# Causal attention in a one-core block: scores from two fp32r parts, two heads in the two halves of the array, and the causal mask as 64-row matmuls

## The reference

```python
xn = _layernorm(x)                                   # x: 4096 tokens x 256
normed = _layer_norm(xn, ln1_g, ln1_b)
q, k, v = normed @ Wqkv + bqkv                       # 16 heads of 16
q, k = rope(q), rope(k)
scores = einsum('bhqd,bhkd->bhqk', q, k) / 4         # causal, 4096 x 4096 per head
attn_out = softmax(scores) @ v
x1 = xn + attn_out @ Wo + bo
s = x1 + gelu(layer_norm(x1) @ W1 + b1) @ W2 + b2
g = silu(moe(xn))                                    # 8 experts, at most 512 rows each, and a shared network
out = x + s * g
```

## Time and profile before

| | us |
|---|---|
| median of 3 runs | 2709.79 |
| lowest and highest | 2703.81, 2711.1 |
| span of the profiled execution, first to last instruction | 2663.3 |
| PE, DVE, ACT, POOL busy | 2394.4, 2072.5, 1463.1, 377.9 |

### The profile page before, as it was taken

The page is one execution under the profiler, slowest core; times in us unless marked ns, Lnnn a source line. Parts: engine busy times, 40 slices in busy tenths (PEclk is TensorE's granted clock), DMA queues, the critical chain, the costliest instruction groups (busy, mean ns, idle before and its releaser), DMA issues. The chain is left out here.

```text
span 2663.3 us, 49751 instructions
## 1 busy us (share of the span) xinstructions
PE 2394.4 (90%) x14968; PEld 1211.4 (45%) x14968; DVE 2072.5 (78%) x3856; ACT 1463.1 (55%) x1762; POOL 377.9 (14%) x319
## 2 busy tenths in 40 slices
PE   0999947999999999998899999999999868886998
PEld 0889942333333333232333333333322247776888
DVE  7888889999999988562799999988864257776776
ACT  2444513566666666777566666666677733332443
POOL 2111149500000000000000000000000023333344
PEclk9999977999999999999999999999999979998999
DMA  4122247300000021000410000003100144443232
GB/s 123 64 95 91 90 114 186 104 9 9 9 9 1 9 50 43 13 10 17 92 30 9 9 9 9 1 9 70 28 9 9 22 115 126 126 126 97 64 95 71
DMA packets 158629, 144.79 MB, mean 54 GB/s; under 512 B 36448, under 2 KB 142176, under 8 KB 158304
## 3 DMA queue, kind: packets, MB, share of 16 engines
q1 hardware_dynamic: 155360, 133.94, 18.9%
q0 software_dynamic: 3072, 8.39, 0.9%
HBM read 95.61 MB, written 46.66 MB: 53 GB/s over the span
## 5 line engine op out<-in xcount | busy, mean ns | idle before, releaser
L883 DVE TENSOR_REDUCE attn_MX<-psB 128x1 f32<-128x512 f32 (+3 forms) x2352 | 1357.2, 638 | 352.5 <-PE psB L756 223.2
L869 ACT ACTIVATE attn_PB<-psB 128x1024 f32<-128x1024 f32 (+3 forms) x1152 | 1035.8, 950 | 563.9 <-PE psB L788 509.7
L756 PE MATMUL psB<-attn_KS,attn_QS 96*128 96x512 bf16 (+3 forms) x2352 | 764.5, 370 | 51.5 <-DVE attn_MX L883 44.9
L788 PE MATMUL psB<-attn_QS,attn_KS 104*128 104x512 bf16 (+3 forms) x2304 | 652.6, 363 | 24.5 <-ACT attn_QS L846 16.0
L803 PE MATMUL psB<-attn_PB,attn_V 128*32 128x512 f32 (+3 forms) x4608 | 579.8, 570 | 0.0
L756 PEld LDWEIGHTS psB<-attn_KS,attn_QS 96*128 96x128 bf16 x2352 | 200.6, 97 | 639.8 <-DVE attn_MX L883 522.2
L788 PEld LDWEIGHTS psB<-attn_QS,attn_KS 104*128 104x128 bf16 x2304 | 210.2, 98 | 336.1 <-ACT attn_PB L869 128.9
L1043 POOL TENSOR_TENSOR W1L<-W,W1H 128x512 fp32r<-128x512 f32 x36 | 53.8, 1524 | 1664.3 <-ACT W1H L1120 1664.3
L803 PEld LDWEIGHTS psB<-attn_PB,attn_V 128*32 128x32 f32 x4608 | 96.3, 108 | 175.9 <-issue 166.8
L759 PE MATMUL psB<-attn_mask_qk,attn_idb 128*128 128x128 bf16 x544 | 119.2, 227 | 0.0
L42 PE MATMUL ps_experts<-W2H,HH_experts 128*128 128x256 f32 x256 | 83.9, 328 | 35.1 <-DVE Y_experts L1233 20.3
(11 more groups left out here) (213 smaller groups left out, 3216.5 us busy)
## 6 DMA issues: line engine op xcount, KB each, us to landing
W<-in_w SPq DMA_DIRECT2D x18, 1024.0 KB, 5.5
attn_KS<-qk_parts SPq DMA_DIRECT2D x240, 64.0 KB, 3.7
attn_QS<-qk_parts SPq DMA_DIRECT2D x210, 64.0 KB, 2.8
qk_parts<-proj_PT SPq DMA_DIRECT2D x32, 384.0 KB, 3.3
attn_V<-v_rows SPq DMA_DIRECT2D x40, 256.0 KB, 4.8
v_rows<-proj_VA SPq DMA_DIRECT2D x32, 256.0 KB, 2.0
XI_experts<-rows_by_place SPq DMA_DIRECT2D x9, 512.0 KB, 6.3
AO_experts<-attention_sums SPq DMA_DIRECT2D x9, 512.0 KB, 6.7
```

The source lines that it names most:

```text
L756: mm = nc.tensor.matmul(ps[:, bank, 0:width], QS[0:MROW, i % 4, h, j * P:(j + 1) * P], KS[w][0:MROW, h, kc * CH:kc * CH + width], start=Tr ...
L788: mm = nc.tensor.matmul(ps[:, bank, r * P:CH], KS[w][0:KROWS, h, kb * P:(kb + 1) * P], QS[0:KROWS, i % 4, h, r * P:CH], start=True, stop=( ...
L869: nc.scalar.activation(PB[:, u % RING, 2 * pair:2 * pair + 2, r * P:CH], ps[:, 2 * (s % 2):2 * (s % 2) + 2, r * P:CH], ACT.Exp, scale=HD * ...
L883: nc.vector.tensor_reduce(MX[:, m % 4, HG * j + h, kc:kc + 1], ps[:, MB + off % 3, 0:w], AX.X, ALU.max).then_inc(reduced, 1)
```

## The change

Parts: q and k are cut into two fp32r parts instead of three bf16 ones, with one copy of ACT and one subtraction of DVE; a score is a sum of three products, 48 rows, and 4 rows for the maximum, 52 in all (`KROWS`). Even heads take rows 0 to 51 of the array, odd heads rows 64 to 115, each half with its own 4 rows for the maximum. The two matmuls of a pair in `scores` are now of two halves; consecutive jobs of maxima also alternate between the halves. The maximum's rows of `QS` are zero until they are set, by a DMA of zeros (two more DMAs in each `load_q`). The ones of `KS` come from a small tile by 8 DMAs instead of POOL. The mask is made by two 64-row bf16 matmuls of 64 columns for each head, in the head's half, instead of one of 128 rows and 128 columns. Jobs on the diagonal of 128 and (for c > 0) 256 keys are made for two heads at once, with one reduction. The constants `TERMS`, `TILE` replace `PAIRS`.

```diff
-PAIRS = ((0, 0), (0, 1), (1, 0), (1, 1), (0, 2), (2, 0))
-MROW = HD * len(PAIRS)
-KROWS = MROW + 2 * HG
+TILE = P // 2
+MROW, MROWS = 32, 4
+TERMS = ((0, 0, 0), (HD, 0, 1), (MROW + MROWS, 1, 0))
+KROWS = HD * len(TERMS) + MROWS
...
+def diagonal_jobs(c):
+    paired = TPC // 2 if c > 0 else 1
+    wide = [(j, (t, t + 2), c) for j in range(paired) for t in range(2)]
+    return wide + [(j, (h,), c) for j in range(paired, TPC) for h in range(HG)]
...
-                        if u < 4:
-                            dve.wait_ge(part1, 4 * c + u + 1)
...
-                            nc.vector.tensor_tensor(RS[:, u % 2, :], ps[:, QTB + u % 2, :], PT[:, u, 0, :], ALU.subtract).then_inc(rest1, 1)
-                        if u > 0:
-                            dve.wait_ge(part2, 4 * c + u)
-                            nc.vector.tensor_tensor(PT[:, u - 1, 2, :], RS[:, (u - 1) % 2, :], PT[:, u - 1, 1, :],
-                                                    ALU.subtract).then_inc(part3, 1)
...
+                        dve.wait_ge(high_made, 4 * c + u + 1)
+                        nc.vector.tensor_tensor(PT[:, u, 1, :], ps[:, QTB + u % 2, :], PT[:, u, 0, :].bitcast(F32),
+                                                ALU.subtract).then_inc(low_made, 1)
...
-        KS = [sb(f"KS{w}", [P, HG, N], BF16) for w in range(2)]
+        KS = [sb(f"KS{w}", [P, 2, N], F32R) for w in range(2)]
-        QS = sb("QS", [P, 4, HG, CH], BF16)
+        QS = sb("QS", [P, 4, 2, CH], F32R)
...
-                    for r, (a, _) in enumerate(PAIRS):
-                        sp.dma_start(QS[HD * r:HD * (r + 1), i % 4, :, :],
-                                     qk[a, 0, bass.ds(group, 1), :, :, c * CH:(c + 1) * CH].rearrange("g d h n -> (g d) h n")).then_inc(q_in[i % 4], 16)
+                    for t in range(2):
+                        for r, a, _ in TERMS:
+                            sp.dma_start(QS[TILE * t + r:TILE * t + r + HD, i % 4, :, :].bitcast(F32),
+                                         qk[a, 0, bass.ds(group, 1), t, :, :, c * CH:(c + 1) * CH].rearrange("g d b n -> (g d) b n")).then_inc(q_in[i % 4], 16)
+                        sp.dma_start(QS[TILE * t + MROW:TILE * t + MROW + MROWS, i % 4, :, :].bitcast(F32).rearrange("p b (x n) -> p (b x) n", n=D),
+                                     zeros_row).then_inc(q_in[i % 4], 16)
...
+                sp.wait_ge(ones_made, 4)
+                for w in range(2):
+                    for t in range(2):
+                        for b in range(2):
+                            sp.dma_start(KS[w][TILE * t + MROW:TILE * t + MROW + MROWS, b, :].bitcast(F32).rearrange("p (x n) -> p x n", n=P),
+                                         ONES[:, b:b + 1, :].broadcast_to([MROWS, NT, P])).then_inc(ones_in, 16)
...
-                for w in range(2):
-                    for c in range(NC):
-                        part = KS[w][MROW:KROWS, :, c * CH:(c + 1) * CH]
-                        nc.gpsimd.memset(part, 0.0).then_inc(consts, 1)
-                        for first in range(2):
...
-                            nc.gpsimd.affine_select(out=part, in_=part, compare_op=ALU.not_equal, fill=1.0, base=-HG * first,
-                                                    pattern=[[-1, HG], [0, CH]], channel_multiplier=1).then_inc(consts, 1)
...
+                    for at, h in enumerate(hs):
+                        rows, b = slice(TILE * (h % 2), TILE * (h % 2) + KROWS), h // 2
+                        mm = nc.tensor.matmul(ps[:, bank, at * width:(at + 1) * width], QS[rows, i % 4, b, j * P:(j + 1) * P],
+                                              KS[w][rows, b, kc * CH:kc * CH + width], start=(at == 0), stop=(kc < c))
...
+                    both = jobs[i % LS][at:at + 2]
+                    for n, job in enumerate(both):
+                        max_job(reads, i, off + n, job, used(n), q_need)
+                    for half in range(2):
+                        for n, job in enumerate(both):
+                            mm = hide_later_keys(off + n, job, half)
+                            if half == 1:
+                                mm.then_inc(maxed, 1)
...
-                    for b in range(2):
-                        h = 2 * pair + b
-                        bank = 2 * (s % 2) + b
-                        mm = nc.tensor.matmul(ps[:, bank, r * P:CH], KS[w][0:KROWS, h, kb * P:(kb + 1) * P],
-                                              QS[0:KROWS, i % 4, h, r * P:CH], start=True, stop=(kb < TPC * c))
-                        if kb >= TPC * c:
-                            mm = nc.tensor.matmul(ps[:, bank, r * P:(r + 1) * P], idb[:, :], mask_kq[:, :], start=False, stop=True)
+                    for t in range(2):
+                        rows = slice(TILE * t, TILE * t + KROWS)
+                        mm = nc.tensor.matmul(ps[:, 2 * (s % 2) + t, r * P:CH], KS[w][rows, pair, kb * P:(kb + 1) * P],
+                                              QS[rows, i % 4, pair, r * P:CH], start=True, stop=(kb < TPC * c))
+                    if kb >= TPC * c:
+                        for half in range(2):
+                            for t in range(2):
+                                rows = slice(TILE * t, TILE * (t + 1))
+                                mm = nc.tensor.matmul(ps[:, 2 * (s % 2) + t, r * P + TILE * half:r * P + TILE * (half + 1)],
+                                                      later_kq[half][rows, :], hide[rows, 0, :], start=False, stop=(half == 1))
```

191 lines of the change are left out of this document (102 added, 89 removed).

## The result

The changed kernel took 2753.74 us (median of 5 runs, 2738.09 to 2793.22) against 2709.79 before (5 runs, 2703.81 to 2715.48): ratio 1.0144, 95% interval 1.0123 to 1.0166. It is slower, 204 us above the forecast and outside its range. Its number is near that of rival B, but B's mechanism isn't there, as the first rows show: that B's number holds is luck.

A forecast was written before the change was run, and what follows sets the result against it. PE was taken as the bound, DVE close behind. Gains of 140 (scores) and 21 (POOL) less 4 (maximum rows) made 157 off span 2663.3, giving 2506; plus 46.5, rounded to 2550 us. Own range 2515 to 2600; wider range 2500 to 2645.

The forecast's parts named there:

- rival B: Score matmuls: the two halves run one after the other, pair 0.454 us; slower, 2750 to 2770 us; chance 12%.
- the sum was -157: Whole kernel: 140 from scores in halves plus 21 from POOL, less 4 for maxima as rows, off the span.
- It doesn't starve behind a group by v: Attention blocks with maxima: DVE's three banks hold 1.8 us, covering PE's 1.1 + 0.23 away plus 0.4 until the first result.
- 53 a pass: Attention steps 0 to 9: us gained in each pass, leaving DVE 10 of its 63 us of idleness.
- 4.5 x 0.598 = 2.69: Full-pace attention block: DVE's reductions need 2.69 us, so DVE becomes the bound.
- The pair at 0.235: Score matmuls: two heads in two halves of the array run at once, 0.235 us a pair against 0.436.
- Steps 10 to 14, 16 a pass: Late attention steps: 9 us gained in blocks with maxima and 7 in those without, each pass.
- POOL, -21: Start of attention: relieving POOL makes DVE's slow routing chain fast, so PE waits less; 21 us gained.
- 8 + 6 more DMAs at 0.47 each: SP's queue ahead of the loads: added DMAs take 6.6 us to issue, and the delay is hidden.
- The median lies 46.5 above this span, and I keep that.: Whole run: 46.5 us between traced span and timed median is added to span 2506, giving 2553.
- Masks at nothing: Mask matmuls: twice as many, of 64 columns instead of 128, in two halves, cost nothing.
- Maxima as rows: Maximum rows: 8 matmuls instead of 4 in each of 32 steps, costing 4 us.

The follow-up runs named there:

- Experiments 1 and 2: Changed kernel with max matmuls reading only upper bf16 halves: 2635.12 us, ratio 0.9731; changed kernel with each block's first score pair issued twice: 2776.14 us, 1.0250.
- rows_left_out: Changed kernel without POOL's 32 indirect row transfers: 2712.33 us, ratio 1.0168 to the kernel before.
- after_again: The changed kernel run once more, unedited, where the kernel before takes 2668.67 us: 2711.46 us, ratio 1.0161.
- before_half_rows: Kernel before, with score and max matmuls over only the upper 40 and 32 of their 104 and 96 rows: 4367.90 us, ratio 1.6127.
- the bf16 kernel: Changed kernel with max matmuls reading only the upper bf16 halves of queries and keys: 2635.12 us, ratio 0.9731; second time 2629.63 us, 0.9719.
- bf16_filled: Changed kernel with bf16 maxima, plus one matmul of 128 rows and 128 columns ahead of each max matmul: 3313.81 us.

## Why the prediction was wrong, by its own steps

Against its own time (both kernels without the crawl) the sum was -157 and the result is +43: 200 us to be found.

- **"It doesn't starve behind a group by v: three banks hold 1.8 us of work, and PE is away for 1.1 + 0.23, plus 0.4 until the first result."** This is the step that failed, and it was called close. The 0.4 and the tenth ahead of the group are the prices of bf16. In fp32r they are 0.43 to the group, 1.00, and 0.49 to the first result: 1.92. That is more than the 1.8 of the three banks, and DVE waits at each group. With bf16 maxima it is 0.33 + 1.00 + 0.40 = 1.73, my own figure, and there DVE's wait is 0.1 a block instead of 0.3. The weight load of the earlier trace rows was "at most 0.12" since it was hidden there; where the matmul waits for a semaphore, its load waits too and shows at 0.18 to 0.19. The forecast had 53 a pass, 106 in all; at full clock the changed kernel has 0 of it. Experiments 1 and 2 show this step. The Trainium skill (TensorE: Matmul & The Clock Gate, Weight-path perf modes) had said that fast loads are off for FP32, and I weighed it only against the pair's spacing. The trace agrees that the fp32r load is the longer one: bf16's is 0.09 to 0.10 here. The 107 ns that I worked out for fp32r were too low against the 0.18 to 0.19 measured.
- **"4.5 x 0.598 = 2.69"** was too small a price for DVE as well. The nine reductions of the earlier trace rows take 5.58, or 0.62 each, and 4.5 x 0.62 = 2.79 is what a block takes with bf16 maxima. Of the 53 a pass some 16 (0.08 for each of 204 blocks) were never to be had.
- **The pair at 0.235** was right: 0.24 here. Rival B is refuted; its 2750 to 2770 held the time by luck.
- **Steps 10 to 14, 16 a pass**: 6. Two blocks without maxima take 4.05 (their exponentials start 0.92, 0.90, 0.92 and 1.31 apart) instead of the 4.25 of the earlier trace rows and the 3.92 of ACT's bound; the others gained less.
- **POOL, -21**: the chain became fast as said (its last operation is over at 389 instead of 412.6), but the load it then waited for came late. "8 + 6 more DMAs at 0.47 each" were eight of 2.1 on average, and drew out the two behind them: PE waited 20.07 for the load, and 7.4 of the 21 stayed.
- **The clock** is in no step. With 106, 20 (32 less 12) and 14 (21 less 7) taken from the 200, 60 are left. That is about what the stretches at a clock below 1.00 have more than before: in `rows_left_out` 26 in steps 0 to 5 of the first pass, 4 in steps 15 and 16, and 30 in steps 1 to 5 of the second. How much of it is the clock alone no run separates. Two traces without the crawl (`rows_left_out` and `after_again`) have 26 and 41 more than before in steps 0 to 5 of the first pass, at the same exponentials (188) and the same busy time of DVE (241.3, 241.5 and 241.9). That the clock is lower there is shown. Which property of the work keeps it down isn't: not masks, not the type, not gaps. The matmuls of 52 rows, where 96 to 104 stood, are the likeliest, by `before_half_rows`; that is argued for the changed kernel and not shown. Rows alone can't be all of it, since the same matmuls are granted 1.00 in step 7 and in steps 10 to 13.
- **"The median lies 46.5 above this span, and I keep that."** It was kept for the wrong reason. The trace of before fits the chips without the crawl (the second one, of 2671.3, repeats its steps), its timed runs those with it. The crawl falls on either kernel, so that keeping the difference did no harm, but it is no constant.
- **Masks at nothing** stays open. All masks together cost some 25 in the bf16 kernel; what they cost in the kernel before wasn't measured, and so the difference isn't known. **Maxima as rows** wasn't tried by itself.

What the crawl is stays open. It comes with POOL's 32 transfers back to back, wherever they stand, on some chips, and not when they are apart; 35 to 40 us. The unedited kernel before was never traced on such a chip. That it crawls there too rests on its times (2707 for 2671) and on `before_half_rows`, which has its program but for the rows and does crawl.

## What to carry to other kernels

Where an engine is fed through a few banks, add up the whole way round (the wait, the weight load, the matmul's own length, the work between) with the prices of the new operand type and for a matmul that has waited: what is hidden in a run of matmuls is not hidden behind a semaphore. A maximum that only shifts a softmax needs no fp32r operands: here it took bf16 ones. An engine's pace is to be read from a long row (0.62 here) and not from its shortest spacing (0.60). When a matmul gets fewer rows, look at the granted clock of each stretch before counting its columns, and ask of a difference between a trace and the timed runs where each was taken before adding it to a forecast.

## What the runs showed of the hardware

- The granted clock stayed at 0.50 for 3,400 us with PE busy for 3,365 of them, when the matmuls of 96 and 104 rows had 32 and 40, in the upper half of the array (`before_half_rows`).
- A weight load is hidden behind the matmul before it in a run of like matmuls. Behind a semaphore it isn't: 0.18 to 0.19 in fp32r, 0.09 to 0.10 in bf16.
- A matmul over all rows between matmuls of 52 costs 0.1 at each change (`bf16_filled`), about the weight load, which starts only then. The Trainium skill (TensorEngine Tiling, Key Properties) says that a change of mode drains TensorE, and the trace agrees: no load is pulled ahead across the change. The 0.1 ahead of each group by v in the kernel before is of the same kind: the group comes 0.32 after the max matmul, whose columns take 0.218, and its own weight load takes 0.106.
- Eight transfers from SBUF to SBUF of 512-byte pieces took 2.1 to 2.3 us each on average to issue, from SP and from ACT alike, and SP's issues of other loads beside them took 2.1 and 2.3 on average instead of 0.47.
- On some chips all other engines nearly stand still while POOL issues indirect transfers one after another (24 matmuls in 35 us), and don't if each is 5 to 6 us behind the last.
